# A state-space block and a coupled feed-forward: GpSimd's share of the products with C placed unit by unit

## The reference, cut to what matters

```python
# x: (16, 1024, 256); DI = 512 channels, N = 16 states
xi, res = split(x @ W_in.T + b_in)            # (16, 1024, 512) each
xi = silu(conv4_causal(xi) + b_conv)
proj = xi @ W_x.T + b_x
delta, B, C = softplus(proj[..., :512]), proj[..., 512:528], proj[..., 528:]
dA  = exp(delta[..., None] * A)               # (.., 512, 16)
dBx = delta[..., None] * B[:, :, None, :] * xi[..., None]
h_t = dA_t * h_(t-1) + dBx_t                  # a scan over the 1024 positions
y_t = sum over n of h_t[.., n] * C_t[n]
y = (y + xi * D) * silu(res)
x = layernorm(x + y @ W_out.T + b_out)
gf = global_net(mean of x over positions)     # 3 layers
for _ in range(3):                            # coupling cycles on out = x
    tf = coupling_net(out)                    # 4 layers, exact gelu
    coupling = 0.1 + range * (0.7 * gf + 0.3 * tf - 0.5) * 2
    out = out + coupling * twist(out)
x = layernorm(x + out)
```

## Time and profile before

| | us |
|---|---|
| median of 3 runs | 4123.83 (4119.0 to 4126.39) |
| the profiled execution | 4114.41 |
| its span, first to last instruction | 4112.6 |
| GpSimd busy | 3643.9 |
| VectorE busy | 3553.5 |
| TensorE busy, matmuls | 3486.1 |
| ScalarE busy | 2757.4 |

### The profile page before, as it was taken

The page is one execution under the profiler, slowest core; times in us unless marked ns, Lnnn a source line. Parts: engine busy times, 40 slices in busy tenths (PEclk is TensorE's granted clock), DMA queues, the critical chain, the costliest instruction groups (busy, mean ns, idle before and its releaser), DMA issues.

```text
span 4112.6 us, 50404 instructions
## 1 busy us (share of the span) xinstructions
PE 3486.1 (85%) x18304; PEld 1587.4 (39%) x18304; DVE 3553.5 (86%) x2784; ACT 2757.4 (67%) x3282; POOL 3643.9 (89%) x1604
## 2 busy tenths in 40 slices
PE   6778988899898888988889898888989888897665
PEld 2224343343434334343443434334343443434232
DVE  0998989998989999899999999999998999989871
ACT  3555858668486776848678585866858677684742
POOL 1998989989899998989989898998989999898961
PEclk9889999999999999989999999999989999998878
DMA  4345364543636454463644536454363645436230
GB/s 145 135 135 184 128 197 137 187 146 122 225 110 202 137 170 149 133 225 109 201 137 142 189 130 203 140 183 149 117 220 115 197 139 171 148 120 226 98 100 26
DMA packets 329127, 629.90 MB, mean 153 GB/s; under 512 B 27440, under 2 KB 226096, under 8 KB 328624
## 3 DMA queue, kind: packets, MB, share of 16 engines
q1 hardware_dynamic: 328880, 626.67, 46.3%
HBM read 456.70 MB, written 169.87 MB: 152 GB/s over the span
## 4 chain that ended last, share of the span: by engine, by line
POOL 54%; issue 14%; DVE 13%; PE 8%; DMA 6%; ACT 5%; SPq 1%; DVEq 0%; POOLq 0%
POOL work L982 32%; POOL work L989 14%; DVE da L902 7%; DMA c_quad<-bc_scratch 3%; POOL oT L998 3%; POOL oT L997 3%; PE banks L569 3%; POOL soft L1004 2%; DVE work L902 2%; PE banks L590 2%; DVE work L910 2%; ACT L705 2%; DMA u_q<-u_scratch 1%; ACT da L758 1%; DMA u_scratch<-soft 1%
## 5 line engine op out<-in xcount | busy, mean ns | idle before, releaser
L982 POOL TENSOR_TENSOR work<-u_q,b_quad 128x1024 f32<-128x1024 f32 x1024 | 2396.7, 2368 | 117.8 <-DMA u_q<-u_scratch 111.9
L902 DVE TENSOR_TENSOR_SCAN da<-da,work 128x1024 f32<-128x1024 f32 x640 | 1462.6, 2285 | 177.7 <-ACT da L758 130.9
L758 ACT ACTIVATE da<-delta_q,neg_a 128x1024 f32<-128x1024 f32 x1024 | 1128.2, 1112 | 693.9 <-DVE work L910 465.4
L989 POOL TENSOR_TENSOR work<-work,c_quad 128x1024 f32<-128x1024 f32 x384 | 907.7, 2364 | 70.1 <-DVE work L902 69.1
L683 PE MATMUL y_sum<-work,v_all 128*32 128x256 f32 x8192 | 632.4, 417 | 387.0 <-POOL work L989 232.8
L902 DVE TENSOR_TENSOR_SCAN work<-da,work 128x1024 f32<-128x1024 f32 x384 | 866.0, 2276 | 36.6 <-ACT da L758 35.8
L910 DVE TENSOR_TENSOR work<-da,c_quad 128x1024 f32<-128x1024 f32 x640 | 782.1, 1222 | 38.2 <-DMA c_quad<-bc_scratch 17.8
L705 ACT ACT_TABLE_LOAD x561 | 719.8, 1283 | 41.7 <-DVE mean_var L875 18.9
L683 PEld LDWEIGHTS y_sum<-work,v_all 128*32 128x32 f32 x8192 | 215.2, 114 | 829.5 <-POOL work L989 297.0
L569 PE MATMUL banks<-xi,w_all 128*128 128x512 f32 x1024 | 475.3, 607 | 5.9 <-ACT big L729 4.7
L556 PE MATMUL banks<-xi,taps 128*128 128x512 f32 (+3 forms) x1024 | 467.3, 605 | 0.4 <-ACT xi L818 0.4
(11 more groups left out here) (73 smaller groups left out, 3146.9 us busy)
## 6 DMA issues: line engine op xcount, KB each, us to landing
delta_q<-delta_scratch SPq DMA_DIRECT2D x256, 512.0 KB, 4.7
u_q<-u_scratch SPq DMA_DIRECT2D x256, 512.0 KB, 6.3
res_scratch<-s_std SPq DMA_DIRECT2D x256, 128.0 KB, 3.2
b_quad<-bc_scratch SPq DMA_DIRECT2D x64, 512.0 KB, 5.8
delta_scratch<-delta SPq DMA_DIRECT2D x64, 512.0 KB, 2.8
u_scratch<-soft SPq DMA_DIRECT2D x64, 512.0 KB, 3.0
c_quad<-bc_scratch SPq DMA_DIRECT2D x64, 512.0 KB, 8.0
s_quad<-res_scratch SPq DMA_DIRECT2D x128, 256.0 KB, 4.5
```

Source lines behind the costliest of these rows:

```text
L758: act.activation(da[:, t % 2, :], delta_q[:, slot, :], ACT.Exp, scale=neg_a[:, t % PERIOD:t % PERIOD + 1]).then_inc(da_ready, 1)
L902: dve.tensor_tensor_scan(dst, da[:, t % 2, :], work[:, slot, :], 0.0, ALU.mult, ALU.add) \
L982: pool.tensor_tensor(work[:, slot, :], u_q[:, copied, :], b_quad[:, j, :], ALU.mult) \
L989: pool.tensor_tensor(work[:, un % WORK, :], work[:, un % WORK, :], c_quad[:, un % PHASE, :], ALU.mult) \
```

## The change

GpSimd's products are given by a list of 20 units of a batch (`POOL_AT`) instead of the alternating pattern of 24. `reduced_at` now works for any list: a unit of GpSimd is reduced two steps late, but no later than the last of its phase. The tables for the side work and for SP's DMAs have other numbers. No instruction's kind or shape is changed.

```diff
-POOL_UNITS = ((1,), (0, 1))
+POOL_AT = (1, 4, 6, 9, 10, 11, 13, 16, 20, 25, 29, 33, 41, 46, 48, 52, 57, 58, 60, 61)
-X_AT = (0, 0, 20, 24, 37, 39, 45, 47)
-V_AT = (2, 5, 28, 28, 41, 41, 51, 53)
-RES_AT = (0, 0, 26, 27, 37, 39, 48, 50)
+X_AT = (0, 0, 20, 24, 38, 39, 45, 50)
+V_AT = (2, 1, 29, 27, 41, 42, 53, 52)
+RES_AT = (0, 0, 27, 27, 38, 39, 47, 50)
-O_AT = (5, 7, 10, 12)
+O_AT = (5, 9, 10, 12)
-F_AT = (-1, 0, 2, 2, 4, 4, 6, 8, 10, 10)
-G_AT = (17, 18, 22)
-E_AT = (59, 61, 61, 62)
+F_AT = (-1, 0, 1, 2, 4, 4, 6, 9, 10, 10)
+G_AT = (16, 18, 23)
+E_AT = (58, 58, 60, 61)
-BC_TAKE = 3
-DELTA_TAKE, DELTA_MAX, U_LAG = 3, 3, 7
-O_STATS, O_RS, O_NORM = 2, 3, 3
+BC_TAKE = 2
+DELTA_TAKE, DELTA_MAX, U_LAG = 3, 3, 6
+O_STATS, O_RS, O_NORM = 3, 4, 4
-MULT_AT, UPD_AT = 11, 14
+MULT_AT, UPD_AT = 11, 15
-DST_AT, UST_AT = (8, 3, 3, 9), (9, 4, 8, 10)
-DLD_AT, ULD_AT = (10, 12, 11, 18), (11, 13, 13, 16)
-SLD, YST = 0, 0
-YGLD_AT = (1, 2, 5, 7)
-RESST_AT = (4, 36, 46, 54)
-X1ST_AT = (12, 13)
-RELOAD_AT, XRES_AT = 52, 63
-OUT_AT = (65, 66)
-XFEAT_AT = 48
+DST_AT, UST_AT = (6, 3, 10, 8), (6, 8, 6, 10)
+DLD_AT, ULD_AT = (10, 12, 13, 17), (12, 16, 16, 17)
+SLD, YST = 2, 0
+YGLD_AT = (2, 2, 2, 8)
+RESST_AT = (16, 35, 47, 51)
+X1ST_AT = (14, 16)
+RELOAD_AT, XRES_AT = 50, 63
+OUT_AT = (64, 69)
+XFEAT_AT = 55
-LB_AT, LC_AT = (52, 55, 59, 60), (60, 62, 63, 62)
+LB_AT, LC_AT = (53, 54, 58, 60), (61, 63, 61, 64)
 def by_pool(u):
-    return u % PHASE in POOL_UNITS[(u // PHASE) % 2]
+    return u % PERIOD in POOL_AT
 def reduced_at(t):
-    units = []
-    late = t - REDUCE_LAG
-    if late >= 0 and late // PHASE == t // PHASE and by_pool(late):
-        units.append(late)
-    if not by_pool(t):
-        units.append(t)
-    return units
+    first, last = t - t % PHASE, t - t % PHASE + PHASE - 1
+    return [u for u in range(first, t + 1) if t == (min(u + REDUCE_LAG, last) if by_pool(u) else u)]
```

## The result

The kernel after takes **4139.3 us** (median of 5 runs, 4133.7 to 4148.4) against 4123.8 (4119.0 to 4126.4) before: ratio 1.0041, 95% interval 1.0027 to 1.0054. It is slower by 0.4%, where 4039 was forecast and 3990 to 4115 was the range.

The account below looks back on a forecast made before the run. GpSimd (89% busy) and VectorE (86%) were taken to share the bound, with VectorE's waits mostly from ScalarE. The terms summed to -5.3 us a batch, 85 over 16 batches, so 4123.8 became 4039; range 3990 to 4115.

Parts of the forecast that it names:

- the batch's start: VectorE's waits of 1.23 us for `work` and 1.95 for TensorE shrink to 0.3 with earlier `u`: -2.9 us a batch.
- C row: Last C row's load, 3.1 us later and wanted at unit 3; with unit 6's product, +0.3 us a batch.
- x7: Last x activation, moved from slot 50 to 53: a new stall makes the scan of unit 56 late, +1.6 us a batch.
- Unit 36: VectorE's own product there gives ScalarE 1.26 us more, so the softplus wait goes from 1.28 to 0.2 us.
- The walk: One batch of the new order followed, with durations from the old trace, to price each wait.
- ScalarE's waits: VectorE's waits for `da` and softplus at units 9, 22, 36, 39, 46, 54: -7.7 us a batch, new ones +1.0.
- GpSimd places: VectorE's waits caused by GpSimd: -1.6 us a batch at unit 32, -2.9 at the batch's start, small ones -1.0.
- the tail: From the last scan to the end, TensorE and ScalarE in turn: no change, with 5 us either way.
- Only the balance changes: Rival: ScalarE's waits stay, only GpSimd's vanish, 4.8 us against 5.0 added a batch; 4127, no change; chance 0.09.
- The C row comes late: Rival: x_feat's load runs into the batch-change DMA train, unit 3 stalls 10.7 us, +4.6 a batch, 4198; chance 0.07.

Follow-up runs that it names:

- e11_three: The kernel after with XFEAT_AT 48, the x7 places back and convolutions v2 and v3 both in slot 28: 4022.3 us, ratio 0.9762 to the kernel before.
- e1_xfeat: The kernel after with only the 1 MB x_feat load back at step 48 instead of 55: 4095.5 us, ratio 0.9937 to the kernel before.

## Why the prediction was wrong

**The step that failed: the batch's start.** The prediction had "chain is u (1521.02), store, `u_q` (1531.95)" and priced the new one with the 8.6 us of the old. It saw the move of x_feat from 48 to 55, but counted its megabyte only behind the chain, as a risk for the C row. SP's order puts it directly ahead of the store of delta, and both stores of the chain land late. Forecast 0.3 of wait, measured 4.80: 4.5 us a batch. Undoing that one number gives back 43.8 us and brings unit 0 to 0.98, with x7 undone too to 0.22. So the rest of the term (one pass less, `u` a slot earlier) holds once the megabyte is away and x7 is back at its place.

**Unit 36.** "The wait of 1.28 for the softplus goes to 0.2": measured 2.57. With the list alone it is 0, so the step's reason (1.26 us more for ScalarE) holds; the tables take it back, since the new places of the two convolutions turn the banks so that TensorE waits 3 us for ScalarE. The walk followed TensorE's order only at x7. 2.4 us a batch; undone, 38.2 us (32 by the ratios). This is the kind of miss that the prediction named as the most likely one, "a stall in TensorE's order that I did not walk into".

**x7.** Forecast +1.6 at unit 55 and 1.2 at unit 54; measured 1.47 and 1.13. Undone, 26.6 us, which is 1.7 a batch. Right. By the Trainium skill (ScalarE: Activation LUTs, What ACT_TABLE_LOAD costs) a drain of 1.38 us would come on top. In the trace of the kernel after, the gelu's activation ends at 1448.32, the load starts at 1448.34 and the next activation at 1449.64. That is 1.32 for the whole switch, with no room for a drain on either side; here the measurement decides.

**ScalarE's waits.** The prediction read 8.6 us a batch for `da` from one form of the scan; with the other form it was 11.1 before, and is 5.2 after. By unit, measured (forecast): 22: 0.58 (0.8), 39: 0.36 (0.5), 48: 0.31 (0.5), 50: 0.29 (0.5), 54 as above, 9: 0 (0). Unit 46 was 1.07 where 0.35 was forecast. It falls to 0.45 when unit 36 is mended, but also to 0.58 when only x7 is (with 2.81 still at unit 36), so its cause stays open.

**GpSimd places.** Unit 32: 0.16 (0). The gate of unit 8: 1.23 with a C row that practically no longer waits (0.1 to 0.2 at units 2 and 3), where 0.8 was meant for both. Right in kind, 0.5 short.

**Once per run.** The first scan of the profiled execution comes at 101.6 us (96.0 before), and its first batch takes 233.4 us (219.8). I had counted this batch as like the others; it is 13.6 longer. From the first scan of the last batch to the end it is 369.8 us instead of 380.9, 11.1 shorter; 3.1 of these lie behind the last scan, inside the 5 us either way that the prediction gave the tail. The four differences (5.6 + 13.6 + 25.9 for the 14 batches between - 11.1) make the 34.0 of the traces. Why the ends differ was not taken apart.

The sum: with the two failed places mended (43.8 + 38.2, an estimate from single gains) the kernel would stand at some 4057, 18 above the forecast; by the ratios (43 + 32) at 4064. Places for that rest are the first batch and units 8 and 46; it was not split among them. The upper bound of 4115 was too low because it priced one further stall at 3 us, and a C row at 1; there were two stalls, of 4.5 and 2.4 us more than forecast.

**The rivals.** "Only the balance changes" (4127) is nearest in number and wrong in mechanism: the waits for ScalarE did fall. The Trainium skill (Perfetto Trace Analysis, Identifying the Most-Contended Engine) would improve the engine with the highest occupancy. By that the change was to give 4121; it measured 4139.3. And VectorE, the busiest engine after it, is busy 226.8 us in a batch shown above of the kernel after and of e11_three alike, while the means of a batch are 8.3 us apart. What decided were the waits. "The C row comes late" put the x_feat load in the right conflict and on the wrong victim.

## What to carry over

When a table moves a large load, ask which small transfer it now stands ahead of, and follow that one to the engine at its end: a load that nothing waits for costs time if a store on the critical chain queues behind it. In a kernel with in-order engines and shared banks, walk every engine whose order the change touches, not only the two that wait; one bank taken in another order cost 32 to 38 us. Undo the rows of a retuned table one by one before judging it: a change that measured +0.4% held -2.4%, and a product list or its tables alone (+1.5%, +2.0%) did not tell what the pair would do.

## What the runs showed of the hardware

**A store behind a load.** The store of delta (512 KB) landed 9.3 us after its issue when a 1 MB load had been issued 0.8 us ahead, and 4.1 us without it (e1_xfeat). Over 13 changes of batch the medians are 8.9 and 4.8 us for the store of delta, and 7.7 and 3.4 us for the store of `u` behind it: some 4 us for one more megabyte. The load itself took 7.6 us (median), and 5.0 in e1_xfeat, where it is issued at another time. The Trainium skill (DMA: Bandwidth & Descriptors, Two DMAs through the same engine are not ordered) says that descriptors of one queue of a DMA engine start in order; the rows agree, but don't show single descriptors.

**A wait of TensorE can cost twice.** The granted clock in 5 us windows ahead of unit 36 in the next batch of the kernel after (columns as in the earlier trace rows), and the rows of TensorE and VectorE there:

```profile
1684.72:1689.72 5.00, 5.00 (x32) 1.85 (x35) 5.00 (x5) 4.68 (x6) 5.00 (x3) 1.00 0.77 273
1689.72:1694.72 5.00, 2.24 (x18) 0.97 (x7) 4.97 (x3) 4.94 (x6) 5.00 (x3) 0.83 0.05 17
1694.72:1699.72 5.00, 5.00 (x11) 2.11 (x10) 4.41 (x4) 4.46 (x5) 5.00 (x4) 0.83 0.54 159
...
1693.17 5.31 PE L631 MATMUL banks<-oT,w_all 128*128 128x512 f32 x8 [2.76 <-ACT big L725]
...
1705.38 0.75 DVE L938 SCALAR_TENSOR_TENSOR delta<-banks,v_all,soft 128x512 f32<-128x512 f32 x1 [2.77 <-ACT soft L856]
```

TensorE stood idle 2.76 us for the bank, and the clock of the two windows is 0.83, part of them at the lower level (1.2 GHz). The eight matmuls behind the wait took 5.31 us here, at a granted clock of 0.69 (window 1693.17:1698.48), where the same eight took 3.70 at 1.00 in the batch shown further up, after a wait of 3.00. VectorE waits 2.77 at unit 36 of this batch, 1.16 in the other: the matmuls' 1.61 us more come back as 1.61 us more of wait. Of batches 2 to 15 of this trace, twelve are like this one and two like the other. So the bank and the order alone cost 1.16 us, and 1.4 of the mean of 2.57 is the lower clock. TensorE's wait was 2.76 to 3.09 us in the twelve and 3.00 to 3.01 in the two, so its length alone does not decide the clock; what does isn't shown.

In the batch of e11_three shown above, the same stretch is granted 1.00 throughout. That batch is its best, with a clock of 0.99 and 208.3 us for TensorE's 1144 matmuls. In the mean of batches 3 to 14 the clock is 0.96 in e11_three and 0.945 in the kernel after, and the matmuls take 213.8 and 216.3 us.
